# A decoder layer on one core: x loaded a second time as columns, a cleared tile multiplied early, roots first on GpSimd, and new orders on four engines

## The chip, the cores and the metric

The kernel runs on one core of one Trainium2 chip. The metric is the time of one execution on the device in microseconds; each kernel has several runs and the median is what counts. The kernel is written in Bass: each engine has an instruction stream of its own, written out by hand, and streams meet only at semaphores.

## The reference, cut to what matters

x is 1024 tokens by 128 channels. Three blocks follow one another, each added to x after a layer norm.

```
a = layernorm(x)
xi = rmsnorm(a @ down_w + down_b)                 # 64 channels, two branches of 32
o1 = window attention of xi[:, :32], windows of 10 tokens, shifted by 5, 8 heads of 4
o2 = window attention of xi[:, 32:], windows of 20 tokens, shifted by 10, 8 heads of 4
p = a + concat(o1 @ proj1, o2 @ proj2) @ up_w + up_b
x = x + p + gelu(rmsnorm(p) @ ffn_w1) @ ffn_w2
x = x + causal attention of layernorm(x) over the first 1024 rows of ctx, k = v = ctx @ Wq.T
f = layernorm(x); router softmax over 8 experts, the two best keep their weight
x = x + shared expert(f) + sum of weight * expert(f)     # 128 -> 256 -> gelu -> 128, 9 in all
```

## The kernel before

Tokens lie in 8 tiles of 128. Most of the work is done in two halves of four tiles, h = 0 and 1; a call such as `values(5)` or `x2_tile(5)` is for one tile. Branch 0 has windows of 10, branch 1 of 20.

The start. x arrives by SyncE's queue in two parts (`PARTS`: tiles 0 to 4 and 5 to 7). VectorE takes moments (`x_moments`), GpSimd raises the variance to the power -1/2 (`rstd0_pow`). TensorE transposes x (`x_columns`, L1290), ScalarE copies it out (`xT_copy`, L568), and `xi_rows` multiplies the columns by the centred down weights. `xi_squares` (VectorE) scales and squares the result, `rstd1_pow` (GpSimd, L449 and L451) gives the second root, `xi_norm` (L898) multiplies by it, and `channels` (TensorE, L1317) transposes into window order. Between `rstd0_pow` and `rstd1_pow` GpSimd does `xn_tiles` (L467), which nothing needs before `xp_add`. `query_centre` and `keys` (TensorE) multiply the context, which arrives later in SyncE's queue.

Window attention, per branch b and half h. `qkv_rows` is many small matmuls (33 rows in, 24 or 48 columns moving). `qkv_copy` brings the result to SBUF. `window_product(b, h, d)` (VectorE, L925) multiplies q and k for d = 0 to 3, the four channels of a head; `qk_sum(b, h, n)` (TensorE, L1266 with half_ident) adds product n into PSUM by an identity matmul, one bank for branch 0 and two for branch 1, and adds the bias after n = 0. `window_scores` (VectorE, L945 and L947) takes the maximum and subtracts it, `window_exp` (ScalarE) the exponential, `window_weighted` (L957) multiplies by v, `value_sum` (TensorE, first_sb) adds over the keys of a window, `window_values` divides, `ox_copy`, `out_columns`, `ot_copy` and `out_project` bring it back to token order, and `xc20_copy`, `xc_add`, `to_tokens`, `xp_add` make p. A product may be written only when `value_sum` of the half before has read its buffer.

`PAIRED` lists the (branch, half) for which VectorE adds products 0 and 1 to products 2 and 3 (`window_pairs`) so that TensorE has two sums and not four; it is empty here. `HALVED` does the like for `value_sum` by `value_add` (L964) in half 1. L1266 is the helper by which all matmuls that aren't transposes are issued; an fp32 matmul has two records in the trace, a bf16 or fp32r one has one.

The rest. `ffn_hidden` and `ffn_output` are the feed-forward, `scores`, `row_max`, `softmax`, `p_columns`, `pT_copy`, `values`, `x2_tile` the cross attention, tile by tile, `x2_moments`, `rstd4_pow`, `x2_norm`, `xf_columns` the last norm. `hidden(h, e, c)` is three fp32r matmuls of 512 columns, with w1 and x each split into a high and a low part (`w1_high` on ScalarE, `w1_low` on GpSimd, L479); `output(h, e)` is 8 fp32 matmuls; `moe_add` (L1131) takes the result out of one of two PSUM banks with the router's weight. `xs_begin` (L462, GpSimd) makes x plus a bias, into which p is added later (`xs_add`, L503).

Every engine does its calls in the order of a list at the end of its block. In TensorE's list the start is

```
centre, x_columns(0), x_columns(1), xi_rows(0), query_centre, keys(0), xi_rows(1), keys(1),
channels(0,0), channels(1,0), qkv_rows(0,0), channels(0,1), channels(1,1), qkv_rows(1,0),
qk_sum(0,0,0), qkv_rows(0,1), qk_sum(1,0,0), proj_up, qk_sum(1,0,1..3), qkv_rows(1,1) first ten,
scores_side(0), qk_sum(0,0,1..3), qkv_rows(1,1) rest, scores_side(1), value_sum(1,0), value_sum(0,0)
```

## Time and profile before

| | |
|---|---|
| runs | 189.1, 189.41, 190.81 us; median 189.41 us |
| span of the profiled execution | 190.2 us |
| TensorE busy | 171.6 us (90%) |
| VectorE busy | 110.4 us (58%) |
| ScalarE busy | 85.9 us (45%) |
| GpSimd busy | 37.5 us (20%) |

The span is that of one execution under the profiler, from its first instruction to its last. It lies 0.8 us above the median of the runs and inside their spread. The profile has for each engine its busy time, for TensorE also the clock that it was granted as a share of full speed, and for each idle stretch who ended it.

### The profile page before, as it was taken

The page shows a single profiled execution, that of the slowest core. Times are in us where ns is not written, and L with a number is a line of the kernel's source. Part 1 is how long each engine was busy: PE and PEld are TensorE (multiplying, and loading weights), DVE is VectorE, ACT ScalarE, POOL GpSimd, SP SyncE. Part 2 cuts the span into 40 slices and gives each one's busy share as a digit, 9 for nine tenths or more (in the row PEclk, how much of TensorE's full clock was granted, in tenths as well). Part 3 has the DMA queues.
Part 4 walks back from the last instruction along what each step waited for, and adds up shares of the span by engine and source line. Part 5 has one row for each costly group of instructions (what it writes and reads, how often), then busy time and mean ns, then how long its engine had stood idle before and what let it go on. Part 6 is the DMA issues. An engine that isn't in the chain of part 4 may idle for free.

```text
span 190.2 us, 3429 instructions
## 1 busy us (share of the span) xinstructions
PE 171.6 (90%) x1322; PEld 138.4 (73%) x1322; DVE 110.4 (58%) x274; ACT 85.9 (45%) x156; POOL 37.5 (20%) x59
## 2 busy tenths in 40 slices
PE   0896799999999998889968799999999999999991
PEld 0762667656699954488855679877899989998991
DVE  6443898005942966997497645747363742923433
ACT  3331730002415713824766485777934356842420
POOL 2695992000000005002027520001021000000000
PEclk9999555559999999999999999999999999999999
DMA  6994000000000000000000000000000001000001
GB/s 182 255 364 182 0 3 5 0 0 3 3 0 0 2 3 0 0 0 0 3 0 2 2 0 0 3 0 0 3 0 0 3 0 57 0 5 0 0 0 55
DMA packets 2588, 5.41 MB, mean 28 GB/s; under 512 B 321, under 2 KB 1835, under 8 KB 2316
## 3 DMA queue, kind: packets, MB, share of 16 engines
q1 hardware_dynamic: 2256, 4.91, 8.2%
q10 hardware_dynamic: 316, 0.29, 0.5%
q8 instruction: 10, 0.16, 0.4%
q14 instruction: 6, 0.05, 0.1%
HBM read 4.67 MB, written 0.52 MB: 27 GB/s over the span
## 4 chain that ended last, share of the span: by engine, by line
PE 74%; DVE 13%; POOL 6%; issue 2%; ACT 2%; DVEq 0%; POOLq 0%
PE ps L1266 69%; POOL xn L467 3%; POOL rstd L451 2%; DVE prod L957 2%; PE ps L1525 2%; DVE xi L898 1%; DVE prod L964 1%; DVE xl L1066 1%; DVE prod L947 1%; DVE stat L945 1%; PE ps L1317 1%; ACT ox L636 1%; DVE xcT L994 1%; DVE hid L867 1%; DVE prT L867 1%
## 5 line engine op out<-in xcount | busy, mean ns | idle before, releaser
L737 ACT ACTIVATE hid<-ps,consts_sb 128x512 f32<-128x512 f32 x36 | 24.2, 686 | 25.5 <-PE ps L1266 25.3
L1266 PEld LDWEIGHTS ps<-moe_w_sb,hid 128*128 128x128 f32 x288 | 34.3, 192 | 1.5 <-issue 0.5
L1266 PE MATMUL ps<-moe_w_sb,hid 128*128 128x128 f32 x288 | 34.8, 275 | 0.0
L1131 DVE SCALAR_TENSOR_TENSOR acc<-ps,wts,acc 128x128 f32<-128x128 f32 x64 | 18.0, 343 | 12.2 <-PE ps L1266 12.1
L1266 PE MATMUL ps<-prod,half_ident 128*128 128x400 f32 x48 | 23.2, 627 | 0.0
L1266 PE MATMUL ps<-xf_hi,w_hi 128*128 128x512 f32 x36 | 16.6, 461 | 0.0
L1266 PE MATMUL ps<-prod,first_sb 128*128 128x200 f32 x90 | 15.7, 334 | 0.7 <-DVE prod L964 0.7
L1266 PEld LDWEIGHTS ps<-prod,first_sb 128*128 128x128 f32 x90 | 15.1, 190 | 1.6 <-DVE prod L964 0.9
L1266 PEld LDWEIGHTS ps<-prod,half_ident 128*128 128x128 f32 x48 | 10.6, 236 | 7.4 <-issue 4.4
L925 DVE TENSOR_TENSOR prod<-qkv 128x400 f32<-128x400 f32 (+1 forms) x16 | 14.7, 976 | 0.0
L1266 PE MATMUL ps<-xf_lo,w_hi 128*128 128x512 f32 x36 | 14.2, 394 | 0.0
L1266 PE MATMUL ps<-xf_hi,w_lo 128*128 128x512 f32 x36 | 14.1, 392 | 0.0
L623 ACT ACTIVATE prod<-prod 128x800 f32<-128x800 f32 (+1 forms) x4 | 2.8, 704 | 23.4 <-DVE prod L947 23.4
L451 POOL TENSOR_TENSOR rstd<-rstd,minus_half 128x1 f32<-128x1 f32 (+3 forms) x16 | 12.9, 809 | 1.3
L449 POOL TENSOR_SCALAR rstd<-mv 128x1 f32<-128x1 f32 (+3 forms) x12 | 2.3, 194 | 54.9 <-DVE mv L1060 32.5
L957 DVE TENSOR_TENSOR prod<-prod,qkv 128x800 f32<-128x800 f32 (+1 forms) x16 | 11.4, 777 | 1.4 <-ACT prod L623 1.4
L449 POOL TENSOR_SCALAR rstd<-ss 128x4 f32<-128x4 f32 (+2 forms) x4 | 0.8, 195 | 52.5 <-ACT sq L663 50.2
L945 DVE TENSOR_REDUCE stat<-ps 128x40 f32<-128x800 f32 (+1 forms) x4 | 3.1, 779 | 13.5 <-PE ps L1266 13.5
L1266 PE MATMUL ps<-v_sb,prT 128*128 128x128 f32 x72 | 9.6, 278 | 1.1 <-DVE prT L1042 1.1
L1266 PEld LDWEIGHTS ps<-v_sb,prT 128*128 128x128 f32 x72 | 8.8, 191 | 1.7 <-issue 1.2
L636 ACT ACTIVATE ox<-vn 32x160 f32<-32x160 f32 (+1 forms) x12 | 4.0, 334 | 12.8 <-DVE vn L977 12.6
L1027 DVE TENSOR_REDUCE nmx<-ps 128x1 f32<-128x128 f32 (+7 forms) x8 | 6.0, 756 | 6.0 <-PE ps L1266 5.9
(156 smaller groups left out, 295.2 us busy)
## 6 DMA issues: line engine op xcount, KB each, us to landing
moe_w_sb<-in_moe_w SPq DMA_DIRECT2D x2, 1152.0 KB, 10.9
pr<-in_ctx SPq DMA_DIRECT2D x1, 576.0 KB, 7.4
out<-acc SPq DMA_DIRECT2D x8, 64.0 KB, 1.6
late_sb<-in_late SPq DMA_DIRECT2D x1, 404.0 KB, 11.4
ffn_hids<-in_bias SPq DMA_DIRECT2D x1, 369.7 KB
x_sb<-in_x SPq DMA_DIRECT2D x1, 320.0 KB, 3.6
x_sb<-in_x SPq DMA_DIRECT2D x1, 192.0 KB, 4.0
first_sb<-in_first ACTq DMA_DIRECT2D x1, 160.0 KB, 3.8
```

The lines of the kernel that those rows point to most:

```text
L451: pool.tensor_tensor(dst, dst, minus_half[:, 0:dst.shape[1]], ALU.pow).then_inc(ready, 1)
L467: pool.tensor_scalar(xn[:, t, :], x_sb[:, t, :], mv[:, t, 0:1], rstd0[:, t:t + 1], ALU.subtract, ALU.mult).then_inc(xn_ready, 1)
L636: act.activation(ox[b][r, 0:w, g * n:(g + 1) * n], vn[b][r].rearrange("p (i c) -> p i c", c=n), ACT.Copy).then_inc(ox_ready[b], 1)
L737: act.activation(hid[:, k % DEEP, c, :], ps[:, c, :], ACT.Gelu, bias=cols_sb[:, i:i + 1]).then_inc(moe_h_ready, 1)
L867: dve.memset(winT[b][C:C + 1, :], 1.0).then_inc(win_clear, 1)
L925: product = dve.tensor_tensor(prod[b][:, d, :].rearrange(SHAPE, i=w, h=nh), spread(q, 1, w), spread(k, 2, w), ALU.mult)
L945: step(dve.tensor_reduce(top, scores.rearrange("p a j r -> p r a j"), AX.XY, ALU.max))
L957: dve.tensor_tensor(prod[b][:, d, :].rearrange(SHAPE, i=w, h=nh), sc[b].rearrange(SHAPE, i=w, h=nh), spread(v, 2, w), ALU.mult).then_inc(w ...
L1027: step(dve.tensor_reduce(nmx[:, t:t + 1], score_cols(t), AX.X, ALU.max, negate=True))
L1131: dve.scalar_tensor_tensor(acc[:, g, :], ps[:, slot_bank(n), t * D:(t + 1) * D], wts[h][:, t, e:e + 1], acc[:, g, :], ALU.mult, ALU.add).t ...
L1266: return pe.matmul(dst, lhs, rhs, start=start, stop=stop)
L1525: last = pe.transpose(ps[:, pT_bank(t, n), (k - a) * P:(k - a + 1) * P], pr[:, t % 2, key_at(t, k):key_at(t, k) + P], ident)
```

## The change

x is also loaded as columns (`x_cols`, 512 KB more, in two transfers each behind its part of x), and `x_columns` and `xT_copy` are gone. A tile of zeros in bf16 (`zeros16`) is cleared on GpSimd first of all; `idle_columns(n)` multiplies it n times, 512 columns each, into a bank that is not in use: 8 times ahead of everything, 1 and 4 times between the two `xi_rows`, 3 times before `qkv_rows` and 4 times between the `channels` of half 1. GpSimd does both `rstd1_pow` before `xn_tiles` and `clear`. `xs_begin` and the three `w1_low` go from GpSimd to VectorE. Half 1 is paired in both branches. The semaphore `win_ready` is split by half. The lists of all four engines are written anew; TensorE now has both `xi_rows` before the `keys`, all eight first sums of half 0 in one piece, and `value_sum(0, 0)` before `value_sum(1, 0)`.

```diff
-PAIRED = ()
+PAIRED = ((0, 1), (1, 1))
...
+        zeros16 = sb("zeros16", [P, 512], BF16)
...
             for n, part in enumerate(PARTS):
+                cols = slice(part.start * P, part.stop * P)
                 sp.dma_start(x_sb[:, part, :], x[:, part, :]).then_inc(ld_x[n], 16)
+                sp.dma_start(xT_sb[:, cols], x_cols[:, cols]).then_inc(ld_xT[n], 16)
             sp.dma_start(consts_sb[:], consts).then_inc(ld_vec, 16)
             sp.dma_start(ctx_sb, ctx).then_inc(ld_ctx, 16)
...
+            pool.memset(zeros16[:], 0.0).then_inc(zeros_clear, 1)
             step(pool.memset(minus_half[:], -0.5))
...
             rstd0_pow(0)
             rstd0_pow(1)
-            xn_tiles()
             rstd1_pow(0)
             rstd1_pow(1)
-            xs_begin()
-            w1_low(0)
-            w1_low(1)
+            clear()
+            xn_tiles()
+            xs_add(0)
+            rstd2_pow(0)
             narrow()
-            clear()
-            rstd2_pow(0)
-            xs_add(0)
...
-            w1_low(2)
...
+            downc_copy()
+            wqc_copy()
             half_copy()
-            downc_copy()
-            xT_copy(0)
-            xT_copy(1)
-            wqc_copy()
             bias_split()
             window_cols(0, 0)
-            w1_high()
+            qkv_copy(1, 0)
             k_copy()
             qkv_copy(0, 0)
             window_cols(0, 1)
             window_cols(1, 1)
-            qkv_copy(1, 0)
+            window_exp(0, 0)
+            w1_high()
             window_exp(1, 0)
+            qkv_copy(0, 1)
...
+            def xs_begin():
+                dve.wait_ge(ld_vec, 16)
+                for n in range(2):
+                    dve.wait_ge(ld_x[n], 16)
+                dve.tensor_tensor(xs[:], x_sb[:], spread(rows_sb[:, R_B2:R_B2 + D], 1, NT),
+                                  ALU.add).then_inc(xs_begun, 1)
+
+            def w1_low(a):
+
+                dve.wait_ge(w1_high_ready, 1)
+                n = EX // W1_CUTS
+                e = slice(a * n, (a + 1) * n)
+                dve.tensor_tensor(w1_lo[:, e], moe_w1_sb[:, e], w1_hi[:, e].bitcast(F32),
+                                  ALU.subtract).then_inc(w1_low_ready, 1)
...
             xi_squares(0)
+            xi_squares(1)
             xi_norm(0)
-            xi_squares(1)
             window_cols20()
+            bias_low()
             xi_norm(1)
+            window_product(1, 0, 0)
             window_product(0, 0, 0)
             window_product(0, 0, 1)
-            bias_low()
             window_product(0, 0, 2)
-            window_product(1, 0, 0)
+            window_product(0, 0, 3)
             window_product(1, 0, 1)
+            window_scores(0, 0)
             window_product(1, 0, 2)
+            window_weighted(0, 0, 0)
             window_product(1, 0, 3)
+            xs_begin()
             window_scores(1, 0)
-            window_product(0, 0, 3)
+            window_weighted(0, 0, 1)
+            window_weighted(0, 0, 2)
+            window_weighted(0, 0, 3)
...
+            window_product(0, 1, 2)
+            w1_low(0)
+            w1_low(1)
+            window_values(0, 0)
...
             window_product(1, 1, 3)
+            window_pairs(1, 1)
             xc_add(0)
-            window_product(0, 1, 3)
             xp_add(0)
+            window_pairs(0, 1)
             window_scores(1, 1)
             xp_norm(0)
+            window_scores(0, 1)
...
             row_max(0)
+            w1_low(2)
+            pT_copy(0)
             row_max(1)
-            pT_copy(0)
...
             row_max(4)
+            pT_copy(4)
             row_max(5)
-            pT_copy(4)
+            x2_tile(4)
+            pT_copy(5)
+            row_max(6)
+            shared_add(0)
             router(0)
-            pT_copy(5)
-            shared_add(0)
-            row_max(6)
...
-            def idle_columns(n):
-
-                pe.wait_ge(cleared, 1)
-                zeros = pu[0][:].rearrange("p i d -> p (i d)")
+            def idle_columns(n, at=6, kept=False):
+
+                pe.wait_ge(zeros_clear, 1)
+                if kept:
+
+                    pe.wait_ge(k_ready, 1)
                 for _ in range(n):
-                    mm(ps[:, 6, :], zeros[:, 0:P], zeros)
+                    mm(ps[:, at, :], zeros16[:, 0:P], zeros16[:])
...
             def xi_rows(n):
-                pe.wait_ge(xT_ready, 2)
+                pe.wait_ge(ld_xT[n], 16)
                 pe.wait_ge(downc_ready, 1)
...
+            idle_columns(8)
             centre()
-            x_columns(0)
-            x_columns(1)
             xi_rows(0)
+            idle_columns(1)
+            idle_columns(4)
+            xi_rows(1)
             query_centre()
+            keys(1)
             keys(0)
-            xi_rows(1)
-            keys(1)
+            channels(1, 0)
             channels(0, 0)
-            channels(1, 0)
+            idle_columns(3, 0)
+            qkv_rows(1, 0)
             qkv_rows(0, 0)
             channels(0, 1)
+            idle_columns(4, 6, True)
             channels(1, 1)
-            qkv_rows(1, 0)
             qk_sum(0, 0, 0)
-            qkv_rows(0, 1)
+            qk_sum(0, 0, 1)
+            qk_sum(0, 0, 2)
+            qk_sum(0, 0, 3)
             qk_sum(1, 0, 0)
-            proj_up()
             qk_sum(1, 0, 1)
             qk_sum(1, 0, 2)
             qk_sum(1, 0, 3)
+            qkv_rows(0, 1)
+            proj_up()
             qkv_rows(1, 1, 0, 10)
+            qkv_rows(1, 1, 10)
+            value_sum(0, 0)
+            value_sum(1, 0)
             scores_side(0)
-            qk_sum(0, 0, 1)
-            qk_sum(0, 0, 2)
-            qk_sum(0, 0, 3)
-            qkv_rows(1, 1, 10)
             scores_side(1)
-            value_sum(1, 0)
-            value_sum(0, 0)
...
             out_project(0, 0)
             qk_sum(1, 1, 0)
+            to_tokens(0)
             qk_sum(1, 1, 1)
-            to_tokens(0)
-            qk_sum(1, 1, 2)
-            qk_sum(1, 1, 3)
             qk_sum(0, 1, 0)
             qk_sum(0, 1, 1)
             h_columns(0)
-            qk_sum(0, 1, 2)
-            qk_sum(0, 1, 3)
...
             ffn_hidden(1, 0)
+            ffn_hidden(1, 1)
             xf_columns(0)
-            ffn_hidden(1, 1)
             xf_columns(1)
             xf_columns(2)
             xf_columns(3)
             ffn_output(1)
+            router_logits(0)
             hidden(0, 0, 0)
...
```

Behind that, in the tails of the lists, the same calls stand in another order, a few places up or down: `hidden` runs further ahead of `output`, and `router(0)` and `shared_add(0)` stand behind `row_max(6)`.

## Rows read from the trace of the kernel before

**Rows 1.** The page, part 2: clock granted to TensorE in 40 slices of the span.
```profile
PEclk9999555559999999999999999999999999999999
```

**Rows 2.** Busy time by stretch: length, PE, PEld, DVE, ACT, POOL, clock, DMA share, GB/s.
```profile
10.00:12.00 2.00, 1.54 (x4) 0.77 (x4) 1.76 (x4) 0.83 (x2) 2.00 (x3) 1.00 0.93 312
...
18.00:20.00 2.00, 1.68 (x22) 1.36 (x21) 1.78 (x4) 1.52 (x2) 0.72 (x2) 0.75 0.00 0
...
40.00:42.00 2.00, 2.00 (x5) 1.01 (x4) 0.00 (x0) 0.00 (x0) 0.00 (x0) 0.50 0.00 0
```

**Rows 3.** Timeline, 0 to 30 us: start, length, engine, line, count, idle before.
```profile
8.95 6.55 POOL L467 TENSOR_SCALAR xn<-x_sb,mv,rstd 128x128 f32<-128x128 f32 x8
...
10.13 0.49 DVE L884 TENSOR_TENSOR xi<-ps,rstd 128x320 f32<-128x320 f32 x1 [3.24 <-issue]
...
14.04 1.85 PE L1266 MATMUL ps<-pr 128*128 128x512 f32 x2
...
17.17 0.49 DVE L898 TENSOR_TENSOR xi<-xi,rstd 128x320 f32<-128x320 f32 x1 [4.82 <-POOL rstd L451]
...
20.42 2.45 DVE L898 TENSOR_TENSOR xi<-xi,rstd 128x192 f32<-128x192 f32 x1 [0.57 <-POOL rstd L451]
...
22.62 4.05 POOL L479 TENSOR_TENSOR w_lo<-moe_w_sb,w_hi 128x768 fp32r<-128x768 f32 x2
22.79 4.31 DVE L925 TENSOR_TENSOR prod<-qkv 128x400 f32<-128x400 f32 x2
...
24.32 3.01 PE L1266 MATMUL ps<-qkvw_sb,prT 33*32 33x24 f32 x160
...
27.25 1.70 PE L1266 MATMUL ps<-prod,half_ident 128*128 128x400 f32 x2
```

**Rows 4.** Timeline, 30 to 75 us.
```profile
37.01 7.20 PE L1266 MATMUL ps<-prod,half_ident 128*128 128x400 f32 x12
...
45.50 1.13 PE L1266 MATMUL ps<-kT,pr 128*128 128x512 f32 x2
...
48.57 1.44 PE L1266 MATMUL ps<-qkvw_sb,prT 33*32 33x24 f32 x80
...
51.04 10.39 PE L1266 MATMUL ps<-prod,first_sb 128*128 128x200 f32 x60
...
66.09 1.51 PE L1266 MATMUL ps<-prod,half_ident 128*128 128x400 f32 x4
...
72.86 0.99 DVE L945 TENSOR_REDUCE stat<-ps 128x40 f32<-128x800 f32 x1 [2.00 <-PE ps L1266]
```

**Rows 5.** The chain that ended last: start, length, what; a late piece.
```profile
168.19 18.22 PE ps L1266 x131
```

**Rows 6.** DMA issues: KB each, us from issue to landing.
```profile
pr<-in_ctx SPq DMA_DIRECT2D x1, 576.0 KB, 7.4
```

**Rows 7.** Groups by line and form: count, busy, mean ns, idle before.
```profile
L1266 PE MATMUL ps<-prod,half_ident 128*128 128x400 f32 x48 | 23.2, 627 | 0.0
...
L957 DVE TENSOR_TENSOR prod<-prod,qkv 128x800 f32<-128x800 f32 x8 | 7.4, 985 | 0.8 <-ACT prod L623 0.8
...
L479 POOL TENSOR_TENSOR w_lo<-moe_w_sb,w_hi 128x768 fp32r<-128x768 f32 x3 | 5.9, 1964 | 0.0
...
L964 DVE TENSOR_TENSOR prod<-prod 128x2000 f32<-128x2000 f32 x1 | 2.2, 2231 | 0.0
```

**Rows 8.** Waits: who waited for whom, us in total, times, longest.
```profile
DVE stat L945 <- PE ps L1266: 13.5, 2, 11.5
...
DVE acc L1131 <- PE ps L1266: 12.1, 8, 2.7
```

**Rows 9.** Timeline, 103 to 108 us.
```profile
103.41 0.84 DVE L1066 TENSOR_SCALAR xl<-acc,mv,rstd 128x128 f32<-128x128 f32 x3
...
104.52 1.75 DVE L1066 TENSOR_SCALAR xl<-acc,mv,rstd 128x128 f32<-128x128 f32 x1 [0.27 <-POOL rstd L451]
...
106.49 1.96 PE L1266 MATMUL ps<-late_sb,ffn_hids 128*128 128x128 f32 x16
```

More of the change, by code:

```diff
@@ L86, in spread, with decoder_layer @@
     return ap.broadcast_to(shape)
-def decoder_layer(nc, x, ctx, first, consts, proj_up, up_w, qkv_w, bias, late, moe_w1, moe_w2,
+def decoder_layer(nc, x, x_cols, ctx, first, consts, proj_up, up_w, qkv_w, bias, late, moe_w1, moe_w2,
                   moe_b2, out):
@@ L254, in decoder_layer @@
         win_ps = [sem("win10_ps"), sem("win20_ps")]
-        win_ready = [sem("win10_ready"), sem("win20_ready")]
+        win_ready = [[sem(f"win{b['w']}_ready_{h}") for h in range(HALVES)] for b in BRANCHES]
         qkv_ps = [sem("qkv10_ps"), sem("qkv20_ps")]
@@ L456, in rstd0_pow @@
                 rstd(rstd0[:, PARTS[n]], mv[:, PARTS[n], 1], 1.0, 1e-5, rstd0_ready)
-            def xs_begin():
-                pool.wait_ge(ld_vec, 16)
-                for n in range(2):
-                    pool.wait_ge(ld_x[n], 16)
-                step(pool.tensor_tensor(xs[:], x_sb[:], spread(rows_sb[:, R_B2:R_B2 + D], 1, NT), ALU.add))
             def xn_tiles():
@@ L582, in window_cols @@
                 dst, src = window_part(b, h)
[L583 removed]
+                act.activation(dst, src, ACT.Copy, scale=cols_sb[0:C, V_N1 + b:V_N1 + b + 1]).then_inc(win_ready[b][h], 1)
             def qkv_copy(b, h):
@@ L1284, in query_centre @@
                 mm(ps[:, 7, DI:DI + P], wqT_sb, down_sb[:, DI:DI + P]).then_inc(wqc_ps, 1)
-            def x_columns(a):
-                pe.wait_ge(ld_down, 16)
-                pe.wait_ge(ld_x[a], 16)
-                for t in range(4 * a, 4 * a + 4):
-                    last = pe.transpose(ps[:, 2 + a, (t % 4) * P:(t % 4 + 1) * P], x_sb[:, t, :], ident)
-                last.then_inc(xT_ps, 1)
             def xi_rows(n):
-                pe.wait_ge(xT_ready, 2)
+                pe.wait_ge(ld_xT[n], 16)
                 pe.wait_ge(downc_ready, 1)
@@ L1670, in _ @@
             scores(0)
+            out_project(1, 1)
+            out_columns(0, 1)
+            p_columns(0, 0)
             scores(1)
-            out_columns(0, 1)
-            out_project(1, 1)
-            p_columns(0, 0)
             out_project(0, 1)
@@ L1706, in _ @@
+            hidden(0, 3, 0)
+            p_columns(4, 1)
             output(0, 1)
-            p_columns(4, 1)
-            hidden(0, 2, 0)
-            hidden(0, 2, 1)
+            values(4)
+            scores(6, 0)
             p_columns(5, 0)
-            values(4)
-            hidden(0, 3, 0)
-            p_columns(5, 1)
-            scores(6, 0)
             scores(6, 1)
             hidden(0, 3, 1)
+            p_columns(5, 1)
+            hidden(0, 4, 0)
+            values(5)
+            output(0, 2)
@@ L1717, in _ @@
             scores(7, 0)
-            hidden(0, 4, 0)
-            output(0, 2)
             p_columns(6, 0)
             hidden(0, 4, 1)
+            hidden(0, 5, 0)
             weight_rows(0)
+            p_columns(6, 1)
             scores(7, 1)
-            p_columns(6, 1)
-            hidden(0, 5, 0)
-            values(5)
+            values(6)
+            output(0, 3)
+            expert_bias(0)
+            p_columns(7, 0)
             hidden(0, 5, 1)
-            expert_bias(0)
-            output(0, 3)
@@ L1744, in _ @@
             xf_columns(7)
             output(0, 6)
+            hidden(1, 0, 0)
+            hidden(1, 0, 1)
             output(0, 7)
-            hidden(0, 8, 1)
-            hidden(1, 0, 0)
+            hidden(1, 1, 0)
+            hidden(1, 1, 1)
+            output(0, 8)
+            hidden(1, 2, 0)
             router_logits(1)
-            hidden(1, 0, 1)
-            hidden(1, 1, 0)
-            output(0, 8)
-            hidden(1, 1, 1)
-            hidden(1, 2, 0)
-            output(1, 0)
@@ L1769, in _ @@
+            hidden(1, 6, 1)
+            output(1, 3)
             output(1, 4)
-            hidden(1, 6, 1)
             hidden(1, 7, 0)
+            hidden(1, 7, 1)
             output(1, 5)
-            hidden(1, 7, 1)
+            hidden(1, 8, 0)
             output(1, 6)
-            hidden(1, 8, 0)
             hidden(1, 8, 1)
```

147 lines of the change are left out of this document (64 added, 83 removed).

## The prediction

> **What bounds the kernel now.** I began with the page: TensorE is busy 90% of the span (table above), and its clock [rows 1] reads half in five slices, about 19 to 43 us. The busy time by stretch places this [rows 2]: 0.75 in 18 to 20 us, so the record of half speed begins at about 19; 0.50 at 40 to 42 with TensorE busy all 2.00 us; the next slice is full again. Before 19 the record says 1.00, but the durations don't bear that out: the 512-column pair took 1.85 us at 14.04 [rows 3] and 1.13 at 45.50 [rows 4], the same kind of matmul. So I take TensorE to have run at 1.2 GHz from its first matmul to about 42.9 us. The Trainium skill says the same of the default state ("TensorE: Matmul & The Clock Gate", part 1: throttled until activity releases it).
>
> Then I read the timeline of the start [rows 3] for what was late. GpSimd's eight xn tiles fill 8.95 to 15.50; only then comes the root that `xi_norm(0)` needs, which waited 4.82 us for it and starts at 17.17. `xi_norm(1)` took 2.45 us for 192 elements although 320 took 0.49, and two products of 400 took 4.31 us, both beside a GpSimd operation with two tensors from SBUF (w_lo, 4.05 us for two). From 24.3 us TensorE is the bound: no idle to 70, and its sums of half 0 run at half speed. In the last part the chain is TensorE alone, 18.22 us in one piece of 131 matmul records [rows 5]; that part can only shrink if it has less work, and it has the same.
>
> **Part by part.** All sums are against the profiled span of 190.2 us; the median of the runs is 0.8 below.
>
> *Start, up to the first window sum (27.25 us before).* With roots first, even if loading x as columns gave nothing, squares begin at 10.13, four steps of 0.49 end at about 12.4, and the root, which took 15.50 to 17.17 = 1.7 us, is there at 14.1 and not at 17.17: 3.1 us earlier. With x as columns, `xi_rows(0)` needs no transposes and copies, and I estimate 12.1. But neither end matters in full, for what is late next is on TensorE: the `keys` stand before `channels`. The context was issued behind two transfers and took 7.4 us, landing at 9.5 [rows 6]; now 512 KB more go ahead of it, at the 312 GB/s of 10 to 12 us [rows 2] 1.65 us, so 11.15. From landing to the first key took 1.3 us before (copy of wqc in it), and two keys at 1.85 make 16.2 us. Then at half speed: ten transposes 1.3, three zero tiles 1.3 (a pass of 512 columns is a quarter of the 1.85, 0.43 with its loads taken off), `qkv_rows(1,0)` 2.8, `qkv_rows(0,0)` 2.5, six transposes 0.8, four zero tiles 1.7: 26.9 us, 0.3 earlier than before. At full speed from about 19 us: `qkv_rows` of branch 1 doesn't scale (160 records in 3.01 us at half [rows 3], 80 in 1.44 at full [rows 4]); branch 0's no row shows at full speed, between 1.25 and 2.5, I take 1.9 (by its neighbour of branch 1 it would be 2.5, by the columns 1.25); transposes 0.6, zero tiles 0.9. That is 24.8 us, 2.4 earlier. VectorE is ready: bias, norms and products have no GpSimd beside them but xn tiles, beside which the 320-element steps took 0.49. Cover gone: the products of branch 0 (0.56 each) start only when `k_copy` and `qkv_copy` are through ScalarE, 0.7 us before the sum.
>
> *Sums of half 0 to the end of `out_project` (27.25 to 66.09).* The work is the same. What of it ran at half speed, 27.25 to 42.9 = 15.65 us, at full speed is: 15 records of 400 columns at 0.33 instead of 0.67 (12 took 7.20, the last three of them at full [rows 4]; 4 took 1.44 at 66.09, start to start), saving 5.0; three bias matmuls, 2.0 to 0.8; `proj_up`, 1.7 to 0.9; `qkv_rows(0,1)`, 2.5 to 1.9. Together 7.6; I take 7.0, since VectorE's chain (score, exponential, weighted) now must keep up: value sums 10.39 us [rows 4] begin about 2 us after the weighted products are ready, by products at 0.98 to 0.99 and 0.5 and scores of 2.0 and 1.15. w1_low (two) and xs_begin add 0.95 x 2 + 1.2 = 3.1 us to VectorE, priced by 985 ns for 800 elements [rows 7]; they stand in its idle time (13.5 us of waiting for sums in all, 11.5 in one piece here [rows 8]). If that cover is gone they cost up to 3.1.
>
> *Contention.* w1_low took 1.96 us each on GpSimd [rows 7] and held up VectorE for 2.1 (`xi_norm(1)`), 3.2 (two products) and 1.4 us (L1066, 1.75 us against 0.84 for three [rows 9]). The first two vanish but were mostly hidden by TensorE. The Trainium skill ("SBUF — State Buffer", the shared port pair) has it that GpSimd and a VectorE operation with two SBUF inputs lock each other out for a whole instruction; the rows agree.
>
> *Pairs in half 1.* TensorE loses 12 of its 48 records [rows 7], 12 x 0.33 = 4.0 us. VectorE gains one operation of 800 (0.99 us) and one of 1600 (between 0.99 and the 2.23 of 2000, 1.8): 2.8 us. On the path: before, from the end of `out_project` to the scores of (1,1) took 66.09 to 72.86 = 6.8 us and VectorE waited 2.00 for TensorE at the end [rows 4]. Now `window_pairs(1,1)` is done before `out_project` ends (products 3.7 after the value sum, pairs 1.8, against out_columns and out_project 6.9), then copy 0.6, `xc_add` 1.3, `to_tokens` 0.6, `xp_add` 0.7, pairs(0,1) 0.95: 4.1 us. Gain 2.7.
>
> *Middle (82 to 108).* `w1_low(2)` leaves GpSimd, and `ffn_hidden(1,1)` no longer waits for `xf_columns(0)`. `ffn_output(1)` began at 106.49 [rows 9] behind the held-up L1066; now it can begin at the second gelu, about 105.0. Gain 1.5 less what `w1_low(2)` costs between row_max(0) and the copy, where VectorE waited 1.3: 1.2 taken, 0 to 1.7.
>
> *Tail.* TensorE's work is the same; the only change can be stalls. `router(0)` (3.0 us) now stands behind `row_max(6)`; `weight_rows(0)` comes some 7.2 us after `scores(6,1)`, and row_max 1.3, shared_add 0.7, router 3.0 and a moe_add 1.1 make 6.1. `hidden(0,4,1)` comes 5.9 us after it, its gelu at 4.6. Both hold by one microsecond. Loss 0 to 2, taken 0.5.
>
> Sum: 2.4 + 7.0 + 2.7 + 1.2 - 0.5 = 12.8 us. 190.2 - 12.8 = 177.4, and 0.8 below for the median: **176.6 us**.
>
> **Rivals.** *The clock doesn't rise before the sums* (28%). For it: in the kernel before, TensorE streamed from 31.7 with little pause and rose only at 42.9; the 8 zero tiles last only 3.4 us, and the rest of the start is small matmuls and transposes with a wait for the context. Sums then begin at 26.9, in one dense piece now, and run some 5 us at half speed before it rises: 2.1 + 2.5 more, 181.2 us. The skill's clock-gate page (part 4, PE-mode transpose) says that transposes don't count as busy; by that rule the transposes between keys and zero tiles would break the dense piece, and this rival is the outcome. No row here shows it.
>
> *The clock rises with the first zero tiles and holds* (15%). Then the keys take 0.97 each start to start and all behind them moves up: 1.8 + 0.6 + 0.6 = 3.0, 173.6 us. Against: TensorE still waits for the context.
>
> *VectorE becomes the bound in half 0* (10%). From `qkv_copy(0,0)` to the end of `out_project` it has 27 us of work against TensorE's 31.7, with three hand-overs to ScalarE of about 1 us. If its 3.1 us of new work isn't covered: 179.7 us.
>
> *The zero tiles and loads do nothing, and the tail stalls: slower* (3%). Mechanism: `output` waits for `moe_taken` of two slots before, and `hidden` runs ahead; if VectorE comes late at each of 17 outputs by over 0.75 us, that eats the 12.8. Its adds waited 12.1 us in all for TensorE [rows 8], so there is slack, and that is why so little. At 1 us each: 193.8 us.
>
> **How the numbers follow.** Forecast 41%, rivals 28, 15, 10 and 3; 3% for less than 1% of change by several small losses. The range leaves out the slower end and the best part of the second rival: 172.5 to 184. Differences under 1% can't be told from none here. Faster by over 1%: 0.94; within 1%: 0.03; slower: 0.03.
>
> **What would show it.** The 512-column pair of the keys: 1.85 us if cold, about 1 if warm. Clock in the stretch of the first sums of half 0: 1.00. First sum at 24.8, `out_project(0,0)` ending at 56, scores of (1,1) at 60, value_sum(1,1) at 70, first hidden at 95, no TensorE idle behind it. VectorE: products of 400 at 0.56 each, w_lo 0.95. The prediction is wrong if the clock reads half behind 27 us, if TensorE waits for weighted products, or if gaps appear before `output` or `weight_rows`.

## The result, and the profile after

The changed kernel takes **184.25 us** (median of 4 runs, 181.98 to 185.52); the kernel before took 190.11 us beside it (4 runs, 189.1 to 191.63). The ratio is 0.959, 95% interval 0.950 to 0.968 (a ratio, here and below, compares only the faster runs of each kernel, so it isn't the quotient of the medians, 0.969). The forecast was 176.6 us in a range of 172.5 to 184.0. It is faster, as forecast, but by clearly less than the 12.8 us: by the medians 5.9 us, with the median 0.25 us above the upper end of the range; by the ratio 7.8 us, to some 182.3 us, inside the range. The profiled execution took 183.42 us with a span of 181.2; it has 1320 matmuls on TensorE, which is busy 166.9 us (92% of the span).

The page, parts 1 and 2 of the changed kernel; in the clock's row each digit is a 40th of the span:

```profile
PE 166.9 (92%) x1320; PEld 135.7 (75%) x1322; DVE 111.2 (61%) x280; ACT 84.6 (47%) x154; POOL 32.0 (18%) x56
...
PEclk9999759956999999999999999999999999999999
```

Before, the row had one dip of five slices [rows 1]. Now it has two shorter ones. Busy TensorE in stretches of one us (length, busy, count, clock, DMA share, GB/s) gives their edges:

```profile
19.00:20.00 1.00, 0.48 (x8) 1.00 0.00 0
20.00:21.00 1.00, 1.00 (x22) 0.51 0.00 0
...
26.00:27.00 1.00, 1.00 (x4) 0.58 0.00 0
...
36.00:37.00 1.00, 1.00 (x17) 1.00 0.00 0
37.00:38.00 1.00, 1.00 (x6) 0.54 0.08 16
...
43.00:44.00 1.00, 1.00 (x5) 0.54 0.00 0
```

So the clock is at 2.4 GHz up to 20.0, at 1.2 until 26.8, at 2.4 until 37.1, and at 1.2 again until 43.9. The record reads 1.00 from the start too, but as in the kernel before the durations say otherwise: the eight zero tiles at 1.30 and the five at 8.04 still take 0.42 to 0.45 us each (in the unpaired version below the same five took 1.24 together), and full speed shows only from the keys on. What TensorE does there, and what the other engines do, is in the timeline, 0 to 45 us (start, length, engine, line, count, idle before):

```profile
1.30 3.60 PE L1267 MATMUL ps<-zeros 128*128 128x512 bf16 x8 [1.30 <-POOL zeros L446]
...
8.04 2.11 PE L1267 MATMUL ps<-zeros 128*128 128x512 bf16 x5
...
11.50 1.95 PE L1267 MATMUL ps<-pr 128*128 128x512 f32 x4 [0.46 <-ACT pr L550]
...
12.30 0.48 DVE L878 TENSOR_TENSOR xi<-xi,rstd 128x320 f32<-128x320 f32 x1
...
14.83 9.07 POOL L466 TENSOR_SCALAR xn<-x_sb,mv,rstd 128x128 f32<-128x128 f32 x8
...
15.12 2.68 PE L1267 MATMUL ps<-qkvw_sb,prT 33*32 33x24 f32 x160
...
19.52 2.09 PE L1267 MATMUL ps<-qkvw_sb,hid 33*64 33x48 f32 x31 [1.02 <-issue]
...
24.51 1.54 PE L1267 MATMUL ps<-prod,half_ident 128*128 128x400 f32 x2
...
34.36 2.52 PE L1267 MATMUL ps<-qkvw_sb,hid 33*64 33x48 f32 x40
...
36.82 1.01 PE L1267 MATMUL ps<-proj_up_sb 32*128 32x128 f32 x4
...
38.27 2.71 PE L1267 MATMUL ps<-qkvw_sb,prT 33*32 33x24 f32 x160
```

Read three things there. The keys' four records start at 11.50 and last 1.95 us; before, two records of the same shape lasted 1.85 [rows 3]. TensorE is at full speed there, earlier than I had said. The root came early: `xi_norm` of 320 elements starts at 12.30 where it was 17.17. And the clock falls in and behind `qkv_rows`, the matmuls of 33 rows and 24 or 48 columns: at 20.0 inside `qkv_rows(0,0)`, half a microsecond behind a gap of 1.02 us, and at 37.1, 0.2 us after the 40 records of `qkv_rows(0,1)`, in the four matmuls of `proj_up` (32 rows). At the second fall TensorE has no gap, neither in 36 to 37 nor in 37 to 38 us. The first sum of half 0 starts at 24.51 and its first two records take 1.54 us: half speed.

The sums and the pairs, 41 to 75 us:

```profile
40.90 11.88 PE L1267 MATMUL ps<-prod,first_sb 128*128 128x200 f32 x60
...
59.45 1.51 PE L1267 MATMUL ps<-prod,half_ident 128*128 128x400 f32 x4
...
62.92 1.94 POOL L493 TENSOR_TENSOR xs<-xs,xp 128x512 f32<-128x512 f32 x1 [39.02 <-DVE xp L996]
...
63.65 0.98 DVE L940 TENSOR_REDUCE stat<-ps 128x40 f32<-128x800 f32 x1
...
66.29 0.76 DVE L1002 TENSOR_TENSOR sq<-xp,rstd 128x512 f32<-128x512 f32 x1 [0.64 <-POOL rstd L456]
```

The 60 value-sum records took 10.39 before [rows 4]. The scores of (1,1) wait for nothing now, where they had waited 2.00 for TensorE. The middle, 93 to 98.5 us, against [rows 9]:

```profile
95.87 1.27 POOL L493 TENSOR_TENSOR xs<-xs,xp 128x512 f32<-128x512 f32 x1
96.01 1.21 DVE L1061 TENSOR_SCALAR xl<-acc,mv,rstd 128x128 f32<-128x128 f32 x1 [0.27 <-POOL rstd L456]
97.44 1.29 PE L1267 MATMUL ps<-late_sb,ffn_hids 128*128 128x128 f32 x10
```

`w1_low(2)` is gone from beside the last normalisation, and `xs_add(1)` stands in its place. And the chain that ended last, a late piece (start, length, what), is still TensorE alone [rows 5]:

```profile
160.45 16.88 PE ps L1267 x125
```

**The sum by stretches**, each from one start to the next in the two traces:

| stretch | before | after | gain | forecast |
|---|---|---|---|---|
| to the first window sum | 27.25 | 24.51 | 2.7 | 2.4 |
| to the end of `out_project` (first record of `qk_sum(1,1)`) | 38.84 | 34.94 | 3.9 | 7.0 |
| to the scores of (1,1) | 6.77 | 4.20 | 2.6 | 2.7 |
| to the end of `value_add(1,1)` | 9.89 | 10.38 | -0.5 | 0 |
| to `ffn_output(1)` | 23.74 | 23.41 | 0.3 | 1.2 |
| to TensorE's last end | 79.91 | 79.87 | 0 | -0.5 |

Together 9.1 of 12.8 forecast (9.0 from the rounded rows), and 9.0 between the spans (190.2 and 181.2). The medians lie only 5.9 apart; why, is said further down, under the median against the span.

### The profile page after: what moved, and what is told of

The parts are those of the page before. It is cut to its first block, busy times and chain, and to the rows that moved or that the text cites. A ratio compares the mean times of both kernels' runs of the same rounds, so it can differ in the third digit from the quotient of the medians.

```text
span 181.2 us, 3426 instructions
## 1 busy us (share of the span) xinstructions
PE 166.9 (92%) x1320; PEld 135.7 (75%) x1322; DVE 111.2 (61%) x280; ACT 84.6 (47%) x154; POOL 32.0 (18%) x56
## 4 chain that ended last, share of the span: by engine, by line
PE 83%; DVE 9%; POOL 2%; issue 2%; ACT 2%; DVEq 0%; POOLq 0%
PE ps L1267 77%; DVE prod L952 2%; PE ps L1521 2%; ACT ox L618 1%; PE ps L1313 1%; DVE prod L959 1%; POOL xs L493 1%; POOL rstd L456 1%; PE ps L1449 1%; DVE xl L1061 1%; DVE acc L1047 1%; DVE xcT L989 1%; DVE vn L972 1%; PE ps L1411 1%; PE ps L1561 0%
## 5 line engine op out<-in xcount | busy, mean ns | idle before, releaser
L1126 DVE SCALAR_TENSOR_TENSOR acc<-ps,wts,acc 128x128 f32<-128x128 f32 x64 | 18.0, 344 | 12.8 <-PE ps L1267 12.4
L1267 PE MATMUL ps<-prod,first_sb 128*128 128x200 f32 x90 | 17.2, 355 | 0.7 <-DVE prod L959 0.7
L920 DVE TENSOR_TENSOR prod<-qkv 128x800 f32<-128x800 f32 (+1 forms) x16 | 11.8, 787 | 9.1 <-PE ps L1267 4.6
L1267 PEld LDWEIGHTS ps<-prod,first_sb 128*128 128x128 f32 x90 | 16.6, 205 | 0.9 <-DVE prod L959 0.9
L1267 PE MATMUL ps<-prod,half_ident 128*128 128x400 f32 x36 | 14.5, 534 | 0.4 <-DVE prod L930 0.4
L952 DVE TENSOR_TENSOR prod<-prod,qkv 128x400 f32<-128x400 f32 (+1 forms) x16 | 11.4, 775 | 0.0
L1267 PEld LDWEIGHTS ps<-prod,half_ident 128*128 128x128 f32 x36 | 7.0, 206 | 5.0 <-issue 1.9
L493 POOL TENSOR_TENSOR xs<-xs,xp 128x512 f32<-128x512 f32 x2 | 3.2, 1604 | 39.0 <-DVE xp L996 39.0
L1267 PE MATMUL ps<-gT,x1T 128*128 128x512 f32 (+3 forms) x24 | 9.6, 490 | 0.0
L1267 PE MATMUL ps<-zeros 128*128 128x512 bf16 x18 | 7.8, 590 | 1.5 <-POOL zeros L446 1.3
L466 POOL TENSOR_SCALAR xn<-x_sb,mv,rstd 128x128 f32<-128x128 f32 x8 | 9.1, 1142 | 0.0
```

The source lines that it names most:

```text
L466: pool.tensor_scalar(xn[:, t, :], x_sb[:, t, :], mv[:, t, 0:1], rstd0[:, t:t + 1], ALU.subtract, ALU.mult).then_inc(xn_ready, 1)
L493: pool.tensor_tensor(xs[:, hs, :], xs[:, hs, :], xp[h][:], ALU.add).then_inc(xs_ready, 1)
L920: product = dve.tensor_tensor(prod[b][:, d, :].rearrange(SHAPE, i=w, h=nh), spread(q, 1, w), spread(k, 2, w), ALU.mult)
L952: dve.tensor_tensor(prod[b][:, d, :].rearrange(SHAPE, i=w, h=nh), sc[b].rearrange(SHAPE, i=w, h=nh), spread(v, 2, w), ALU.mult).then_inc(w ...
L1126: dve.scalar_tensor_tensor(acc[:, g, :], ps[:, slot_bank(n), t * D:(t + 1) * D], wts[h][:, t, e:e + 1], acc[:, g, :], ALU.mult, ALU.add).t ...
L1267: return pe.matmul(dst, lhs, rhs, start=start, stop=stop)
```

## The experiments

The open question: where did the 3.1 us of the second stretch go, and which parts of the change made the gain? The theory was that the small matmuls of `qkv_rows` let the clock fall (and that the roots carry the start); the rivals were that the zero tiles decide the clock, that VectorE's new work (3.1 us) holds up half 0, and that the second load of x or the pairs carry the gain. Every version ran beside the kernel before on the same chip (its medians 190.68, 191.22 and 191.05 us).

**The changed kernel again.** No edit.

> The changed kernel once more, unaltered, as the yardstick for the other three on the same chip. All theories: 182 to 186 us, 0.96 to 0.975 of before, with the clock falling twice, once in the small matmuls of half 0 and once in those of half 1, at times that shift from run to run.

Measured: 184.44 us (6 runs, 182.12 to 186.94), ratio 0.963 (0.953 to 0.973). In this execution the clock fell three times, at 23.0, at 40.1 (this time inside `qkv_rows(1,1)`) and, new, at 70.8 until 77.6. The keys ran at half speed here, zero tiles or not, and the first sum started at 26.45. Timeline, and busy TensorE by stretches of one us:

```profile
12.35 3.75 PE L1267 MATMUL ps<-pr 128*128 128x512 f32 x4 [0.46 <-ACT pr L550]
```

```profile
69.00:70.00 1.00, 0.37 (x4) 1.00 0.00 0
...
71.00:72.00 1.00, 1.00 (x2) 0.50 0.00 0
```

The stretch from `value_add(1,1)` to `ffn_output(1)` took 25.3 us and not 23.4: the third fall costs 1.9. So one kernel has more than one course of the clock, and medians closer than about 1% aren't told apart here.

**No zero tiles** (twice; the tiles are only filler, no result depends on them):

```
-            idle_columns(8)
-            idle_columns(1)
-            idle_columns(4)
-            idle_columns(3, 0)
-            idle_columns(4, 6, True)
```

> The changed kernel without any of the 21 multiplications of the cleared tile; all else as changed. Clock theory: the clock was up for the keys only because of the first 8 tiles, so the keys take 1.85 us each and not 0.43 per record, and the rise at the sums comes later by at least the 2.8 us of tiles that were there; the keys, the transposes and the first sums cost 2 to 4 us more, 185 to 188 us. Rival (order alone): the tiles do nothing for the path, the clock rises in the dense sums anyway and the time stays at 182 to 184 us, or 1 us less.

> The changed kernel without any multiplication of the cleared tile, once more, to have a profile and runs in which the clock behaves as usual. From the runs so far: keys at 1.85 us each, first sum within 1 us of the changed kernel's, because 4.3 us of tiles at half speed are gone too; total within 1 us of the changed kernel. Rival, that the tiles pay: 2 us or more longer.

Measured: first 185.87 us (4 runs: 183.04, 184.1, 187.63 and one of 271.78), ratio 0.975 (0.961 to 0.989); then 183.96 us (6 runs, 182.45 to 185.23), ratio 0.968 (0.959 to 0.976). The one execution of 271.78 us was the one profiled: its clock is 0.50 to 0.56 from 13.7 us to the end, mean 0.57, span 269.5. Page, part 2, of that execution:

```profile
PEclk9955555555555555555555555555555555555555
```

The second trace had the usual course, keys at half speed and a fall at 18.9 that ends at 25.7. Timeline:

```profile
10.79 3.75 PE L1267 MATMUL ps<-pr 128*128 128x512 f32 x4 [0.46 <-ACT pr L550]
...
23.20 1.67 PE L1267 MATMUL ps<-prod,half_ident 128*128 128x400 f32 x2
```

Four records of the keys take 3.75 us against 1.95 in the profiled execution of the change. But the tiles bring the clock up for the keys only in some executions: of ten traces of the changed kernel and its variants that have them, six have the keys at 1.95 or 1.96, one at 3.53, and three at 3.75, as without. And where the clock is up it is lost again around `qkv_rows`, the first sum starts at 23.20 without tiles and at 24.51 with them, and the second median is no worse. The tiles bought nothing that can be measured here. Whether they guard against the long execution stays open: it came once in 10 runs without them, never in 10 of the changed kernel; the kernel before, which multiplies no tiles, never had it either (39 runs).

**Pairs undone:**

```
-PAIRED = ((0, 1), (1, 1))
+PAIRED = ()
-            window_pairs(1, 1)
-            window_pairs(0, 1)
+            qk_sum(1, 1, 2)
+            qk_sum(1, 1, 3)
+            qk_sum(0, 1, 2)
+            qk_sum(0, 1, 3)
```

> The changed kernel with all four sums of half 1 on TensorE again (no pairs on VectorE). Theory of the pairs: the stretch from the end of out_project to the scores of branch 1, half 1 grows by the 2.5 us that it lost, of the 4.0 us that the 12 records cost; total 2 to 3 us more. Rival: VectorE is the bound there, so that its 2.8 us of pair sums balance the saving, and the time stays within 0.7 us.

Measured: 184.79 us (4 runs, 183.62 to 186.07), ratio 0.981 (0.970 to 0.993). The scores wait for TensorE again:

```profile
64.99 0.99 DVE L940 TENSOR_REDUCE stat<-ps 128x40 f32<-128x800 f32 x1 [3.34 <-PE ps L1265]
```

From `qk_sum(1,1)` to these scores it took 6.73 us against 4.20: the pairs are worth 2.5 us in their stretch. What reaches the whole time is not settled: the medians show 0.4 to 0.5 us of it, the ratios (0.981 against 0.959 and 0.963, intervals overlapping) up to 4. The clock did not fall a third time in this trace (its second fall was 36.0 to 42.8); the sums keep TensorE working where, with pairs, it waits. The other traces point the same way: of ten with half 1 paired (the long one left out) seven have the third fall, of three without pairs (this one, the kernel before, and the zero tiles alone, below) none. And the mean clock of the four unpaired runs is 0.958 to 0.972, that of the changed kernel's ten 0.931 to 0.969. So the pairs may give part of their gain back by a third fall; that they cause it is not shown, since three paired traces wait there too and keep the clock.

**Work back on GpSimd:** `xs_begin`, `w1_low(0)` and `w1_low(1)` behind the xn tiles, `w1_low(2)` behind `rstd4_pow(3)`.

```
+            xs_begin()       # GpSimd's list, behind xn_tiles()
+            w1_low(0)
+            w1_low(1)
-            xs_begin()       # VectorE's list
-            w1_low(0)
-            w1_low(1)
-            w1_low(2)
```

> The changed kernel with xs_begin and the three w1_low on GpSimd again, behind xn_tiles. Theory of cover: VectorE was idle where it did them, and the port conflict now falls on window scores and weighted products between 24 and 33 us and on x2_norm at 96 us: 1 to 3 us more, most of it at the norm (L1061 grows to about 1.8 us) and before the value sums. Rival: TensorE covers it all, within 0.5 us; or VectorE is freed by 3.1 us and the kernel gains up to 1 us.

Measured: 183.65 us (4 runs, 182.63 to 183.78), ratio 0.973 (0.965 to 0.982). VectorE is held up again, for all that. Timeline:

```profile
21.62 2.33 POOL L477 TENSOR_TENSOR xs<-x_sb,consts_sb 128x1024 f32<-128x1024 f32 x1
...
22.45 4.29 DVE L924 TENSOR_TENSOR prod<-qkv 128x400 f32<-128x400 f32 x5 [2.25 <-ACT qkv L591]
...
95.89 1.80 POOL L485 TENSOR_TENSOR w_lo<-moe_w_sb,w_hi 128x768 fp32r<-128x768 f32 x1
...
96.03 1.74 DVE L1065 TENSOR_SCALAR xl<-acc,mv,rstd 128x128 f32<-128x128 f32 x1 [0.27 <-POOL rstd L456]
```

The five products take 4.29 us against 3.10 in the changed kernel, and the normalisation 1.74 against 1.21. Neither can be seen in the median: the first is hidden by TensorE, the second is 0.5 us. The Trainium skill ("SBUF — State Buffer", section "Who interferes with whom") has it that a VectorE instruction with two SBUF inputs contends with a GpSimd instruction that reads SBUF; the five products, with two inputs each, beside `xs_begin` (2.33 us) agree. The normalisation has one tensor input, so that sentence doesn't cover it, but it was held all the same, until `w1_low(2)` ended: 96.03 + 1.74 against 95.89 + 1.80.

**xn tiles first, roots behind:**

```
+            xn_tiles()
             rstd1_pow(0)
             ...
-            xn_tiles()
```

> The changed kernel with GpSimd's xn tiles ahead of the roots again. Theory of the start: xn tiles end near 15.6 us, the root of part 0 at 17.3, so the first transposes start at 17.8 and not at 13.3; the whole start is 4 to 4.5 us later, and TensorE, idle from 13.4 on, also gets a lower clock: total 4 to 6 us more. Rival: since the sums of half 0 began only 2.7 us earlier than before, the root was worth at most 3 us and the total grows by 1 to 3.

Measured: 188.37 us (10 runs, 186.7 to 191.97), ratio 0.993 (0.989 to 0.998). Timeline of the start:

```profile
8.94 6.53 POOL L466 TENSOR_SCALAR xn<-x_sb,mv,rstd 128x128 f32<-128x128 f32 x8
...
17.13 0.51 DVE L878 TENSOR_TENSOR xi<-xi,rstd 128x320 f32<-128x320 f32 x1 [4.51 <-POOL rstd L456]
...
29.64 1.44 PE L1267 MATMUL ps<-prod,half_ident 128*128 128x400 f32 x2
```

The wait of [rows 3], 4.82 us for the root, is back (4.51), and the first sum starts 5.1 us later. With everything else of the change in place, this one exchange of two calls takes away 4 of the 5.9 to 6.8 us that the change gains by the medians. It is its largest part.

**Zero tiles alone, in the kernel before:** 8 ahead, 5 before `query_centre`, 4 between channels of half 1, the three into another bank left out.

```
+            idle_columns(8)
+            idle_columns(5)
+            idle_columns(4, 6, True)
```

> The kernel before with one part of the change alone: the cleared tile in bf16, multiplied 8 times ahead of everything, 5 times before query_centre and 4 times between the two channels of half 1 (the 3 into bank 0 are left out). Clock theory: the keys at least in some runs take half their time (records of 0.43 us), but the small matmuls behind them bring the clock down again, so that most of the sums of half 0 still run at half speed until about 40 us: within 1.5 us of before, either way. Rival: once up, the clock stays up and the kernel gains 5 to 7 us.

Measured: 193.2 us (4 runs: 189.22, 193.11, 193.28, 193.32; no ratio) beside 191.05 (11 runs, 188.51 to 192.56). Two records of the keys took 1.10 us there, where two had taken 1.85 [rows 3], then TensorE waits for `xi`:

```profile
10.22 1.10 PE L1269 MATMUL ps<-pr 128*128 128x512 f32 x2 [0.46 <-ACT pr L567]
...
17.76 2.32 PE L1322 MATMUL ps<-first_sb,xi 128*32 128x128 f32 x10 [4.92 <-DVE xi L901]
```

Without the roots, the clock won at the keys is lost in a wait of 4.92 us (it falls at 15.75). Tiles alone show no gain.

**x loaded once**, transposed on TensorE as before:

```
-                sp.dma_start(xT_sb[:, cols], x_cols[:, cols]).then_inc(ld_xT[n], 16)
+            xT_copy(0)       # ScalarE's list
+            xT_copy(1)
+            x_columns(0)     # TensorE's list, behind the first zero tiles
+            x_columns(1)
```

> The changed kernel without the second load of x: TensorE transposes and ScalarE copies as before the change, 512 KB less to load. Theory of the queue: the keys wait for the context, which now lands about 1.5 us earlier, and the transposes fit into the wait; keys start at 10.0 to 10.5 us and not 11.5, the root of part 1 comes 1.5 us later, the first sum moves by less than 1 us, and the total by under 1 us either way. Rival: the second load was worth its 2 us at the squares, so first sum and total come 1.5 to 2 us later.

Measured: 183.84 us (6 runs, 182.31 to 184.94), ratio 0.967 (0.959 to 0.975). The keys start at 11.62, as late as with the second load (11.50):

```profile
11.62 1.96 PE L1273 MATMUL ps<-pr 128*128 128x512 f32 x4 [0.46 <-ACT pr L550]
```

The second load neither gains nor costs anything measurable. Two starts of the keys don't settle what it does to the context, though: in the traces with the second load they start anywhere from 10.16 to 12.46.

**`qkv_rows` apart.** The next three test the clock. First, the small matmuls of half 1 were separated by sums:

```
             qk_sum(1, 0, 1)
+            qkv_rows(0, 1)
             ...              # qk_sum(1,0,2), (3), proj_up
-            qkv_rows(0, 1)
+            scores_side(0)
             qkv_rows(1, 1, 0, 10)
-            qkv_rows(1, 1, 10)
+            scores_side(1)
             value_sum(0, 0)
+            qkv_rows(1, 1, 10)
             value_sum(1, 0)
-            scores_side(0)
-            scores_side(1)
```

> The changed kernel with the small matmuls of half 1 no longer in one piece: qkv_rows(0,1) between the second and third sum of branch 1, the two parts of qkv_rows(1,1) behind scores_side(0) and behind value_sum(0,0), both scores_side ahead of the value sums. The work is the same. Clock theory: the clock no longer falls at about 37 us, so that the first 3 us of value sums run at full speed; from the first sum to the end of out_project 34.9 becomes 33 to 33.5 us, total 1.5 to 2 us less than the changed kernel. Rival: the fall has nothing to do with the small matmuls (or VectorE's weighted products set the start of the value sums), and the stretch stays within 0.5 us.

Measured: 186.38 us (6 runs, 185.22 to 187.61), ratio 0.980 (0.972 to 0.988). Busy TensorE by stretches of one us, and its timeline:

```profile
40.00:41.00 1.00, 1.00 (x59) 1.00 0.00 0
...
45.00:46.00 1.00, 1.00 (x12) 1.00 0.00 0
...
58.00:59.00 1.00, 1.00 (x6) 0.50 0.00 0
```

```profile
56.72 1.64 PE L1267 MATMUL ps<-late_sb,ox 128*128 128x32 f32 x10 [1.80 <-ACT ox L618]
```

As the theory has it, the clock is full in 37 to 47 us, 59 small matmuls in one stretch among them. But the order put `scores_side` and the last value sum later, TensorE waits 1.80 us for `ox_copy`, and the clock falls there instead (57.5 to 61). The stretch from the first sum to the end of `out_project` is 35.9 us: the clock as the theory has it, the order a bad one.

Second, the same with `qkv_rows(1,0)` of the start split by zero tiles:

```
-            qkv_rows(1, 0)
+            qkv_rows(1, 0, 0, 10)
+            idle_columns(2, 1)
+            qkv_rows(1, 0, 10)
+            idle_columns(2, 1)
```

> The kernel with the small matmuls of half 1 spread out, and with two cleared-tile multiplications in the middle of qkv_rows(1,0) and two behind it, 0.9 us of added work at full speed. Clock theory: the clock also holds through the first half's rows, so transposes, zero tiles and the first 2.3 us of sums run at full speed: 2.5 us saved less 0.9 spent, 1 to 2 us less than with the rows spread alone. Rival: the tiles are too few to hold it, the clock falls at 19 to 21 us all the same and the total is 0.9 us more.

Measured: 189.38 us (6 runs, 186.18 to 192.02), ratio 0.986 (0.975 to 0.997). A miss:

```profile
22.00:23.00 1.00, 1.00 (x22) 1.00 0.07 16
...
24.00:25.00 1.00, 1.00 (x10) 0.50 0.00 0
```

The clock still falls at 23.1, in the small matmuls of branch 0, and returns only at 30. Two tiles at two places do not hold it. With the rows of half 1 apart as in the first, it then stays up until 60.7.

Third, the separation of the first, with `scores_side` left behind and VectorE's order fitted to it:

```
             qk_sum(1, 0, 1)
+            qkv_rows(0, 1)
             ...
-            qkv_rows(0, 1)
             qkv_rows(1, 1, 0, 10)
-            qkv_rows(1, 1, 10)
             value_sum(0, 0)
+            qkv_rows(1, 1, 10)
-            window_scores(1, 0)             # VectorE
             window_weighted(0, 0, ...)      # three calls
+            window_scores(1, 0)
```

> The changed kernel with the small matmuls of half 1 split up (qkv_rows(0,1) between the sums of branch 1, the second half of qkv_rows(1,1) behind value_sum(0,0)), scores_side left behind the value sums, and VectorE's last three weighted products of branch 0 ahead of window_scores(1,0). Clock theory with the hand-over kept covered: no second fall of the clock; first sum to the end of out_project 33 to 33.5 us and not 34.6 to 34.9; total 1 to 2 us less than the changed kernel, 182.5 to 183.5. Rival: the fall still comes (5 us of small matmuls and tiny ones remain side by side), or value_sum(1,0) now waits for its weighted products: the stretch stays at 34.5 or grows.

Measured: **181.85 us** (6 runs, 180.6 to 182.83), ratio 0.957 (0.948 to 0.966), the fastest version of all; the changed kernel's ten runs took 181.98 to 186.94, and the intervals of the ratios overlap. The clock in the rows of half 1:

```profile
37.00:38.00 1.00, 1.00 (x72) 1.00 0.00 0
...
72.00:73.00 1.00, 1.00 (x7) 0.50 0.00 0
```

and the value sums around them:

```profile
38.03 3.65 PE L1267 MATMUL ps<-prod,first_sb 128*128 128x200 f32 x20
...
42.98 7.04 PE L1267 MATMUL ps<-prod,first_sb 128*128 128x200 f32 x40
...
56.66 1.51 PE L1267 MATMUL ps<-prod,half_ident 128*128 128x400 f32 x4
```

3.65 + 7.04 = 10.7 us for the 60 records that took 11.88, and the stretch from the first sum to the end of `out_project` is 33.41 us against 34.94. In this execution the fall in the rows of half 1 is gone; those at 18.7 and at 66.5 remain. Three of its six runs took 180.6 to 181.0 us at a mean clock of 0.978 to 0.989, three 182.7 to 182.8 at 0.959 to 0.967: 2 us between them, about what the third fall was worth above (the next version, which differs in two calls of GpSimd alone, was slower again). Only the profiled one, of the second group, can be read in that detail.

**And the root of the block ahead of `xs_add(0)`**, on top of it:

```
-            xs_add(0)
             rstd2_pow(0)
+            xs_add(0)
```

> The same, and on GpSimd rstd2_pow(0) ahead of xs_add(0). Theory: the 1.94 us of xs_add no longer stand before the root that xp_norm(0) needs, and from the scores of branch 1, half 1 to the end of the pair sum of its weighted products 10.4 us go back to 9.9: 0.5 us less than the kernel above. Rival: xs_add then runs beside VectorE's weighted products and holds them up by its port, no gain.

Measured: 183.55 us (6 runs, 181.72 to 186.14), ratio 0.965 (0.957 to 0.974). From the scores to `value_add(1,1)` 10.67 us, against 10.38. Timeline:

```profile
64.67 1.27 POOL L493 TENSOR_TENSOR xs<-xs,xp 128x512 f32<-128x512 f32 x1
...
64.73 1.76 DVE L1002 TENSOR_TENSOR sq<-xp,rstd 128x512 f32<-128x512 f32 x1
```

The normalisation no longer waits for the root and lasts 1.76 us and not 0.76, beside the add: the wait has become contention, and nothing is won.

This trace also bears on the three before it, for TensorE's order is the same as in the version above. Here the clock did fall a second time, at 38.6 until 42.1, behind 80 small matmuls and in the value sums of branch 0, which took 5.33 us and not 3.65:

```profile
38.27 5.33 PE L1267 MATMUL ps<-prod,first_sb 128*128 128x200 f32 x20
```

```profile
38.00:39.00 1.00, 1.00 (x26) 0.82 0.00 0
```

The stretch from the first sum to the end of `out_project` took 34.39 us, against 33.41 in the version above and 34.94 in the changed kernel. So keeping the rows apart makes the second fall rarer in these traces, and doesn't prevent it: of four executions with the rows of half 1 apart, three had none before 57.5; of the seven with them together in the changed order (the long one left out) every one had it, between 36.0 and 44.5.

## Why the prediction was right or wrong

**Bound, direction and tail: right.** TensorE is still the chain's end, the piece behind `ffn_output(1)` takes 79.87 against 79.91 us, and the late `router` and outputs cost nothing of the 0.5 that I took.

**Start: right in size (2.7 for 2.4), partly for another reason and partly by luck.** The roots do it: xn tiles first puts the first sum back by 5.1 us. The size is that of one execution: in the traces with the same start (the repeat, the unpaired version and three of the last four) the first sum starts between 23.25 and 26.69, where before it was 27.25. The terms of the forecast, too, add up to 26.6 and 25.0 us and not to 26.9 and 24.8. The first key record came at 11.50 against 11.03 before, less than the 1.65 us that I had counted for the 512 KB ahead of the context, but by the spread of its start above one trace doesn't price that load. The keys ran at full speed, as in the second rival ("rises with the first zero tiles"), but it did not hold.

**First sum to the end of `out_project`: 3.9 for 7.0, the step that failed.** It rests on "at full speed from about 19 us", and its own sign of being wrong came true: the clock reads half behind 27 us. The clock was up earlier than that and fell again at 20.0, in `qkv_rows(0,0)`, so the sums began at half speed at 24.51 after all; that is the first rival, "the clock doesn't rise before the sums", with its rise at 26.8 and not 5 us into them. Then it fell once more at 37.1, behind the first rows of half 1, which no case of mine had. I had worked out 7.6 us and kept 0.6 back, so 3.7 are to be explained, and rows price 3.8: 1.2 for the sums of 24.51 to 26.8 at half speed (half of the 2.3 us), 1.5 for the 60 value-sum records (11.88 against 10.39), 0.5 for `proj_up`, which took 1.45 us from 36.82 to 38.27 where I counted 0.9, and 0.6 for `qkv_rows(0,1)`, which took 2.52 us where I took 1.9. For that one I gave the bounds 1.25 and 2.5: it doesn't scale with the clock, like its neighbour of branch 1. That the clock was at half in these stretches and what it cost is read from the rows; that the small matmuls bring it down is supported and not shown: with the rows of half 1 apart three of four executions had no fall there, and the fastest version had 1.5 us less in this stretch, but in the fourth it fell at 38.6 all the same.

**VectorE as the bound (rival three): no.** With its new work back on GpSimd the median was 183.65 and not clearly another: the 3.1 us were covered, as I had said.

**Pairs: right (2.6 for 2.7), 2.5 when undone.** How much of it reached the whole time is open: 0.4 us by the medians, up to 4 by the ratios.

**Scores to `value_add(1,1)`: -0.5 for 0, missed.** I had not looked at what GpSimd would do there: `xs_add(0)`, 1.94 us, stands ahead of the root in GpSimd's list and now falls into that stretch. Swapping the two did not mend it.

**Middle: 0.3 for 1.2, mis-sized.** The cover named there, `w1_low(2)` gone from GpSimd, was right; what was late next was not followed: `xs_add(1)`, 1.27 us, runs beside the last `xl` (1.21 against 0.84 for three of its kind without company [rows 9]).

**The median against the span: wrong.** I took the median 0.8 below the span of before. The time lies above the span, by 1.8 us in most executions of before (190.72 with 188.9, 188.06 with 186.3; 1.75 to 2.0 in all), so that the profiled execution of 190.2 was one of some 192 us; and by 2.2 to 2.5 for the changed kernel (183.42 with 181.2). The forecast should have been 177.4 + 2.2 = 179.6. So of the 7.7 us between 176.6 and the median, 3.0 are this step, 3.8 the gains of the stretches (12.8 against 9.0), and 0.8 the distance of the profiled run from its own median.

**The Trainium skill's rule on transposes** ("TensorE: Matmul & The Clock Gate", part 4, PE-mode transpose), which stood with the first rival, isn't borne out or refuted: the fall at 20.0 came in small matmuls 5 us behind ten transposes, and no run separates the two; the one at 37.1 has no transpose in the 12 us before it. Part 1 of the same page of the Trainium skill describes a default that is throttled until activity releases it; the keys of the version without tiles, 3.75 us against 1.95, agree.

**Open.** Why the clock falls a third time in some executions and not in others: TensorE waits there in all traces with pairs, and seven of ten have the fall. Why it falls a second time in one of two versions with the same order on TensorE. Whether the one execution of 271.78 us has to do with the tiles. And no order was found that keeps the clock up in the rows of half 0.

## What to carry to other kernels

Count a clock gain only over stretches whose matmuls you have seen run at full clock: behind a stream of small matmuls TensorE can be busy without a gap and still lose it. Spreading them among dense sums kept it in three executions of four here; check that nothing waits for what was moved back, and look at more than one execution before you count on it. When a root of a few columns and a batch of big tiles share an engine, put the root first; it was 4 us of 190 here, more than filler, loads and moved work together. Where something leaves an engine from beside a critical operation, look up what that engine runs next: it will stand there.

## What the hardware showed that I had not expected

The clock falls while TensorE is busy without a gap: at 37.1 us after 36.00 to 37.00 with busy 1.00, just behind matmuls of 33 rows; 40 records of 48 columns took 2.52 us at full clock and 2.57 at half (29.22 us in the kernel before). One execution stayed at 0.50 to 0.56 of the clock from 13.7 us to its end and took 271.78 us. The moment of each rise and fall shifts by 3 us or more between executions of one kernel (second fall at 37.1 and 40.1), and with it the time: the kernel before ran in 188.1 to 192.6 us. And the time outside the span went from 1.8 to 2.2 us and more with the change. It is not the zero tiles (1.8 in the kernel before with tiles) and not the second load (2.2 to 2.5 without it); with the work back on GpSimd it is 1.8 to 2.1, so what moved to VectorE bears on it, and how stays open.
